# Six waits for TensorE instead of four in a tile's gathers (recommendation model, one core)

## The reference

```python
h = relu(dense @ dw1 + db1)                       # 2048 x 13 -> 64
dense_emb = relu(h @ dw2 + db2)                   # 64 -> 64
sparse_emb = emb_tables[f_ids, sparse_idx]        # 2048 x 26 x 64, clamped indices
emb = concatenate([dense_emb[:, None], sparse_emb], axis=1)
inter = einsum('bfd,bgd->bfg', emb, emb)          # 27 x 27 per row: the gram
pairs = inter[:, iu0, iu1]                        # its 351 pairs above the diagonal
z = concatenate([emb.reshape(2048, -1), pairs], axis=1)
z = relu(z @ ow1 + ob1)                           # 2079 -> 512
z = relu(z @ ow2 + ob2)                           # 512 -> 256
z = relu(z @ ow3 + ob3)                           # 256 -> 128
return z @ ow4 + ob4                              # 128 -> 1
```

## Time and profile before

| | before |
|---|---|
| time, median of 3 runs | 543.22 us (543.18 to 543.4) |
| profiled execution: span | 704.8 us (the page gives it no other time) |
| PE busy | 484.0 us (69%) |
| GpSimd busy | 392.8 us (56%) |
| VectorE busy | 151.4 us (21%) |
| ScalarE busy | 148.4 us (21%) |
| mean granted clock of PE | 0.818 of full speed |
| moved by DMA | 19.39 MB, 28 GB/s |

### The profile page before, as it was taken

The page is one execution under the profiler, slowest core; times in us unless marked ns, Lnnn a source line. Parts: engine busy times, 40 slices in busy tenths (PEclk is TensorE's granted clock), DMA queues, the critical chain, the costliest instruction groups (busy, mean ns, idle before and its releaser), DMA issues.

```text
span 704.8 us, 5797 instructions
## 1 busy us (share of the span) xinstructions
PE 484.0 (69%) x2262; PEld 265.8 (38%) x2262; DVE 151.4 (21%) x295; ACT 148.4 (21%) x334; POOL 392.8 (56%) x420
## 2 busy tenths in 40 slices
PE   4864928659286693938759487693937938597788
PEld 1223414334143342424334243342414423254666
DVE  1021302122030221402222030320402213131223
ACT  2312203121111312203122121212203122121312
POOL 6756464764647466564764647466464665647330
PEclk9986967959589596977959789596976979779799
DMA  8522231221313222131221213223231231322110
GB/s 250 98 20 23 19 23 15 26 22 17 22 15 26 20 19 23 18 23 16 24 23 17 22 16 26 20 19 22 18 24 16 21 22 18 22 18 26 12 14 2
DMA packets 17167, 19.39 MB, mean 28 GB/s; under 512 B 7359, under 2 KB 8386, under 8 KB 17127
## 3 DMA queue, kind: packets, MB, share of 16 engines
q0 software_dynamic: 13312, 13.66, 23.2%
q1 hardware_dynamic: 3408, 5.02, 2.1%
q10 hardware_dynamic: 420, 0.34, 0.2%
HBM read 18.99 MB, written 0.01 MB: 27 GB/s over the span
## 4 chain that ended last, share of the span: by engine, by line
another core or an unknown queue 42%; PE 34%; DVE 11%; issue 9%; ACT 4%; DMA 0%; DVEq 0%
PE l_ps L678 9%; PE gram_ps L657 8%; PE l_ps L686 8%; DVE slots L291 4%; DVE gram_c L315 2%; PE l_ps L669 2%; PE tr_ps L640 1%; DVE feat L282 1%; DVE pairs L296 1%; PE l_ps L772 1%; PE tr_ps L621 1%; DVE h1t L303 1%; ACT slots L443 1%; ACT gram_c L455 1%
## 5 line engine op out<-in xcount | busy, mean ns | idle before, releaser
L247 POOL DMA_INDIRECT emb<-table_dram,rows x416 | 392.6, 944 | 287.1 <-issue 117.0
L678 PE MATMUL l_ps<-w_sb,feat 128*128 128x512 f32 x390 | 197.9, 656 | 13.9 <-DVE feat L282 7.2
L657 PE MATMUL gram_ps<-slots 64*128 64x108 f32 x960 | 88.8, 352 | 144.1 <-DVE gram_c L315 139.5
L657 PEld LDWEIGHTS gram_ps<-slots 64*128 64x128 f32 x960 | 81.6, 258 | 161.7 <-DVE gram_c L315 145.0
L678 PEld LDWEIGHTS l_ps<-w_sb,feat 128*128 128x128 f32 x390 | 77.6, 209 | 120.8 <-issue 110.5
L315 DVE COPY gram_c<-gram_ps 32x432 f32<-32x432 f32 x60 | 36.5, 609 | 343.4 <-remote 275.5
L455 ACT COPY gram_c<-gram_ps 32x432 f32<-32x432 f32 x60 | 30.5, 508 | 305.5 <-remote 262.8
L686 PE MATMUL l_ps<-w1p_sb,pairs 118*128 118x512 f32 x90 | 53.4, 740 | 14.4 <-DVE pairs L296 11.9
L621 PE MATMUL tr_ps<-ident_sb,emb 128*128 128x128 f32 x203 | 36.6, 291 | 23.9 <-DMA emb<-table_dram,rows 13.5
L443 ACT COPY slots<-tr_ps 64x256 f32<-64x256 f32 (+1 forms) x128 | 50.3, 393 | 1.1
L621 PEld LDWEIGHTS tr_ps<-ident_sb,emb 128*128 128x128 f32 x203 | 26.6, 149 | 53.8 <-issue 35.9
(11 more groups left out here) (103 smaller groups left out, 202.9 us busy)
## 6 DMA issues: line engine op xcount, KB each, us to landing
emb<-table_dram,rows POOLq DMA_INDIRECT x416
w_sb<-ow_dram SPq DMA_DIRECT2D x3, 1024.0 KB, 7.4
w1p_sb<-ow_pairs_dram SPq DMA_DIRECT2D x1, 708.0 KB
w_sb<-ow_dram SPq DMA_DIRECT2D x1, 512.0 KB
w_sb<-ow_dram SPq DMA_DIRECT2D x1, 256.0 KB
idx_raw<-idx_dram ACTq DMA_DIRECT2D x1, 208.0 KB, 2.7
w1d_sb<-ow_dram SPq DMA_DIRECT2D x1, 128.0 KB
w_sb<-ow_dram SPq DMA_DIRECT2D x1, 128.0 KB
```

The lines of the kernel that those rows point to most:

```text
L247: pool.indirect_dma_start(out=emb[:, t % RING, c // 2, c % 2 * D:(c % 2 + 1) * D], out_offset=None, in_=table, in_offset=bass.IndirectOffs ...
L657: mm = nc.tensor.matmul(gram_ps[:, bank, r * GCOLS:(r + 1) * GCOLS], x.rearrange("p c f -> p (c f)"), x[:, :, 0:SLOTS], start=True, stop=True)
L678: nc.tensor.matmul(l1_ps[t % 2][:], feat[t % 2][:, n - 1, :], w1_sb[:, n - 1, :], start=False, stop=False)
```

## The change

The waits in front of the gathers are laid out anew, from tile 1 on. Group 0 keeps its wait. In the middle of group 0, after 4 of its 8 gathers, stands what was in front of group 1 (all groups of the tile before are transposed). In front of group 1 GpSimd waits for the first half of the gram of the tile before. In the middle of group 1 stands what was in front of group 2 (group 0 of its own tile is transposed). In front of group 2 it waits for the second half of the gram of the tile before. Group 3 keeps its wait. The gathers, their order and all other engines are as before.

```diff
                 for n, (a, b) in enumerate(GROUPS):
                     if t >= 1:
-                        pool.wait_ge(transposed, t * NG + (-2, 0, 1, 2)[n])
+                        if n == 0:
+                            pool.wait_ge(transposed, t * NG - 2)
+                        elif n == 1:
+                            pool.wait_ge(gram_done, 2 * t - 1)
+                        elif n == 2:
+                            pool.wait_ge(gram_done, 2 * t)
+                        else:
+                            pool.wait_ge(transposed, t * NG + 2)
                     for c in range(2 * a, 2 * b):
+                        if t >= 1 and c == 2 * a + 4 and n < 2:
+                            pool.wait_ge(transposed, t * NG + n)
                         pool.indirect_dma_start(
```

## The result

The changed kernel takes 561.9 us (561.0 to 562.8, 4 runs) beside 543.3 us for the kernel before: ratio 1.034, 95% interval 1.033 to 1.035. It is slower, as forecast, but by 18.6 us where 7 were forecast.

A forecast was written before the change was run, and what follows sets the result against it. GpSimd was taken as the bound: 416 gathers 1.249 us apart, no slack. The wait for gram half 0 would open 0.9 us late in 8 tiles, adding 7 us to the 543.2 us median: 550 us, range 542.8 to 562.

The forecast's parts named there:

- GpSimd is the bound, with 1.249 us a gather and no slack: Timed runs: GpSimd's gathers, 32.46 us a tile, set the time, with PE waiting some 5 us a tile.
- The one gate that matters is gram half 0 ahead of group 1: Start of group 1: of the waits, only this one, opening at E + 9.48 against E + 10.29, could cost time.
- 0.8 us to spare at full clock: Start of group 1: the gate opens 0.8 us before GpSimd comes, 0.3 us where the features begin later.
- E: End of group 3's second gather in a tile, the point from which GpSimd's arrivals and gate openings are counted.
- S: Start of PE's transpose of group 3, put at E + 2.45 us when PE waits for that gather.
- One such stretch costs 1.70 us: Features and gram after PE's pause: low clock costs 1.70 us, so the gate opens 0.9 us late.
- I take 8 of the 12: Of the 12 tiles where GpSimd is the bound, 8 have a late gate, 0.9 us each, 7 us in all.
- the two counts weighed: Tiles with a late gate: 8, as forecast, or 12 by the skill's clock rule, 11 us, 554 us.
- Middle of group 1: hidden, 1.6 us: Wait for group 0's transposes of its own tile: opens at E + 13.3, GpSimd there at E + 15.3; costs nothing.
- Tiles 13 and 14 as PE's own: In tiles 13 and 14 PE is the bound, 33.9 us against 32.46; GpSimd's loss there doesn't count at the end.
- The long hole ... will be there again: Profile after: the delay between gram half 0 and its copies returns, span some 2.5 us a tile longer, about 740 us.
- The step that set the hole aside for the timed runs: The 13.6 us hole behind gram half 0 belongs to the profiled execution; the forecast stands on the timed median, 543.2 us.

The follow-up runs named there:

- e1: The kernel before, unchanged, profiled anew: 543.15 us, ratio 1.000, span 542.1 us.
- e8: The kernel before with only the waits that the ring of four tiles needs: 543.4 us, ratio 1.000.
- e2: The kernel before plus only the wait for gram half 0 ahead of group 1: 565.6 us, ratio 1.041.
- e3: The changed kernel without the wait for gram half 0, the five other waits kept: 545.8 us, ratio 1.0045.
- e13: The changed kernel with the wait for gram half 0 one gather earlier, before the last gather of group 0: 572.2 us, ratio 1.053.
- e12: The kernel before plus only the wait in the middle of group 1, for group 0's transposes of its own tile: 545.6 us, ratio 1.0042.
- e10: The kernel before plus only the wait in the middle of group 1, on a chip where the kernel before took 707 us: 641 us, ratio 0.905.
- e11: The changed kernel with the wait for gram half 0 one gather earlier, on the chip where the kernel before took 707 us: 643 to 660 us.

## Why the prediction was right in its way and wrong in its size

- **GpSimd is the bound, with 1.249 us a gather and no slack.** Right: e1 and e8.
- **The one gate that matters is gram half 0 ahead of group 1.** Right: e2 has the loss with it alone, e3 loses it without it.
- **0.8 us to spare at full clock.** Right: 0.4 us late when it is put one gather earlier (e13), open at the gate of tile 14 in the changed kernel, behind features of 4.46 us. The 2.45 us from E to S in it held too, at 2.39 to 2.60 us in PE's tiles 0 to 13.
- **"One such stretch costs 1.70 us".** This is the term that failed. It was taken from the six matmuls of `pairs1` behind pauses that add up to 1.85 us. Ahead of the 11 late gates the low clock lay over nearly 5 us of the features: the ten took 6.94 to 7.33 us in place of 4.56, some 2.5 us lost. In tile 4 they lose 2.47 us, which makes the gate late by 2.47 - 0.82 = 1.65 us in the prediction's sum, and by 1.76 us as measured (E + 12.05 against E + 10.29), twice the forecast 0.9. The trace of the kernel before had such a price too, which the prediction has only as "about 4.5 us or more": behind pauses of 2.10 and 0.65 us the same six matmuls took 5.49 us, 2.65 us more than at full clock:

```profile
541.75 5.49 PE L686 MATMUL l_ps<-w1p_sb,pairs 118*128 118x512 f32 x6 [0.65 <-DVE pairs L296]
```

  What sets how long the clock stays low isn't shown. The length of the pause alone doesn't: in e1, 3.81 and 1.44 us were followed by features of 6.05 us, and 2.00 and 1.69 us by 7.22.
- **"I take 8 of the 12".** Too few: 11 tiles, those behind a short upper stage or none among them. A late gate also lengthens PE's next pause, ahead of group 2: from 3.68 us in e1 to 4.67 in tile 4, and from 2.00 to 2.80 in tile 5. That this keeps the loss alike from tile to tile is likely, but not shown. The Trainium skill ("TensorE: Matmul & The Clock Gate", section on what is actually happening) has only activity release the clock; of the two counts weighed, the one by that rule, 12, came nearer. With 2.47 us and 11 tiles the prediction's own sum is 11 x 1.65 = 18.2 us in place of 8 x 0.9; the rows have 19.2.
- **"Middle of group 1: hidden, 1.6 us".** Only at full clock. With the features at low clock and a long upper stage it is 0.4 to 1.2 us late in three tiles of e3, and 0.3 to 1.1 us in four, 2.6 us in all, when it stands alone (e12). In the changed kernel it shows no loss, as GpSimd has by then already waited at the gram gate.
- **Tiles 13 and 14 as PE's own.** Not as put: in the changed kernel GpSimd still loses 1.67 us at tile 13's gate, and in e2 1.5 us at tile 14's, and the time follows the whole sum.
- **"The long hole ... will be there again", a span near 740 us.** Wrong: see the last section. The step that set the hole aside for the timed runs held; taking it for something of profiled executions didn't.

What stays open: why e2, with fewer waits, is 4 us slower than the full change. The largest part is the gate of tile 14, ahead of which the features of tile 13 took 6.15 us in e2, behind a pause of 2.01 us, and 4.46 us in the changed kernel, behind one of 1.55. Whether that pause decides wasn't tried, nor what makes GpSimd start 0.78 us after the gram's end in e2 and 0.28 us after it in the changed kernel.

## What to carry to other kernels

An engine that sets the time has no slack: each wait put in its way has to be costed against the path that opens it at that path's slow clock, not at its fast one. TensorE's pauses ahead of a gate are part of the gate's price, and they cost nothing only as long as nobody waits for the work behind them. To place such a wait, count in steps of the waiting engine: here two gathers later it was free, and one gather later it still cost 1%.

## What the runs showed of the hardware

One chip ran all three kernels tried on it much slower, with the hole of the first profile. In the batch of e10 and e11 the kernel before took 707 us (703 to 719, 7 runs), where three other chips gave 543.1 to 543.4. The waits of e10 there, and its timeline at one gram:

```profile
DVE gram_c L317 <- remote: 192.5, 16, 13.6
ACT gram_c L457 <- remote: 179.9, 16, 13.1
...
244.64 1.03 ACT L457 COPY gram_c<-gram_ps 32x432 f32<-32x432 f32 x2 [12.86 <-remote]
244.64 1.23 DVE L317 COPY gram_c<-gram_ps 32x432 f32<-32x432 f32 x2 [13.55 <-remote]
245.09 0.94 POOL L249 DMA_INDIRECT emb<-table_dram,rows  x1 [3.17 <-PE tr_ps L623]
```

Its first gram half ends at 234.80 + 2.04 = 236.84, and the copies begin 7.8 us later, on both engines at once. The same kernel has no such wait on another chip (e12). So the first profile, with its 704.8 us, was in all likelihood of a chip of that kind, and the median beside it of another; which chips these were isn't known. A span far from the median can be another chip and need not be the profiler. On that chip the added waits helped: e10 took 641 us and e11 643 to 660 us, ratios 0.905 (0.900 to 0.911) and, by its two shorter runs, 0.915 (0.906 to 0.924), where the same two kernels cost 0.4% and 5.3% elsewhere. What delays the copies there, and whether the whole change gains there too, wasn't tried.
